# A factorization-machine tower on one core: the last K-tile of field pairs goes into spare rows and one fp32r product

## The reference, cut to what matters

```python
x0 = xk = e                      # (1024, 39, 16)
for W in (f0, f1, f2):           # (39*39, 128), (128*39, 128), (128*39, 128)
    z = einsum('bfd,bgd->bfgd', x0, xk).reshape(b, f*g, d)
    cur = einsum('bpd,pm->bmd', z, W)
    outs.append(cur); xk = cur
z = sum(concatenate(outs, 1), -1)            # (1024, 384)
h = relu(concatenate([z, dense_ctx], 1) @ W_top1 + b_top1)
h = relu(h @ W_top2 + b_top2)
y = h @ W_top3
```

## Time and profile before

| | |
|---|---|
| three runs | 1340.83, 1345.21, 1346.58 us (median 1345.21) |
| the profiled execution, its own time | 1342.32 us |
| its span in the trace | 1340.6 us |
| TensorE busy | 1273.5 us, 95% |
| VectorE, ScalarE, GpSimd busy | 1080.1, 1050.1 and 662.9 us |
| granted TensorE clock, mean over the span | 0.985 |

### The profile page before, as it was taken

How to read it: one execution, slowest core, us unless ns; L and a number is a source line. 1 busy time by engine, 2 the same in 40 slices (tenths; PEclk the granted TensorE clock), 3 DMA queues, 4 the chain that set the end, 5 groups by cost and what they waited for, 6 DMA issues and landing times. The chain is left out here.

```text
span 1340.6 us, 21409 instructions
## 1 busy us (share of the span) xinstructions
PE 1273.5 (95%) x6680; PEld 978.8 (73%) x6680; DVE 1080.1 (81%) x2285; ACT 1050.1 (78%) x3363; POOL 662.9 (49%) x634
## 2 busy tenths in 40 slices
PE   1389999999999999999999999999999999999998
PEld 0347777777777777777777777877777777777787
DVE  2059989988889888788878888798887888788884
ACT  2048888888888888788878888888887888788884
POOL 7777556654545547454566545455474532333100
PEclk9679999999999999999999999999999999999999
DMA  6082012100311003110211103111031102110000
GB/s 142 11 235 54 26 52 73 52 28 3 99 32 44 28 22 91 47 32 14 73 51 51 29 4 94 36 44 29 17 92 51 31 13 70 49 49 27 1 1 1
DMA packets 51178, 63.60 MB, mean 47 GB/s; under 512 B 13068, under 2 KB 24345, under 8 KB 51020
## 3 DMA queue, kind: packets, MB, share of 16 engines
q1 hardware_dynamic: 34544, 56.08, 13.7%
q0 software_dynamic: 10128, 2.98, 2.1%
q10 hardware_dynamic: 6392, 3.18, 1.0%
HBM read 11.08 MB, written 1.02 MB: 9 GB/s over the span
## 5 line engine op out<-in xcount | busy, mean ns | idle before, releaser
L538 ACT ACTIVATE scaled_x<-Y,x_col 128x128 f32<-128x128 f32 x3072 | 929.7, 506 | 190.6 <-PE Y L844 178.7
L842 PE MATMUL Y<-f_high,cur_high 128*128 128x512 f32 (+1 forms) x1280 | 603.7, 472 | 3.7 <-DVE sum_b L688 2.0
L843 PE MATMUL Y<-f_low,cur_high 128*128 128x512 f32 (+1 forms) x1280 | 499.0, 390 | 0.0
L844 PE MATMUL Y<-f_high,cur_low 128*128 128x512 f32 (+1 forms) x1280 | 499.0, 390 | 0.0
L427 POOL TENSOR_TENSOR pairs<-shifted,base 117x512 f32<-117x512 f32 x186 | 241.7, 1301 | 436.6 <-PE C L770 434.7
L688 DVE SCALAR_TENSOR_TENSOR sum_a<-Y,x_col,sum_a 128x128 f32<-128x128 f32 x768 | 264.9, 345 | 155.4 <-PE Y L844 153.3
L391 POOL DMA_INDIRECT rows<-in_tbl_dram,ids_sb x312 | 306.9, 984 | 77.5 <-issue 66.2
L842 PEld LDWEIGHTS Y<-f_high,cur_high 128*128 128x128 f32 x1280 | 241.3, 189 | 95.9 <-issue 37.5
L843 PEld LDWEIGHTS Y<-f_low,cur_high 128*128 128x128 f32 x1280 | 242.1, 189 | 86.3 <-issue 52.1
L707 DVE TENSOR_REDUCE cur<-scaled_x 128x128 f32<-128x1920 f32 x128 | 275.6, 2153 | 15.0 <-ACT scaled_x L538 1.6
L844 PEld LDWEIGHTS Y<-f_high,cur_low 128*128 128x128 f32 x1280 | 240.7, 188 | 51.0
(11 more groups left out here) (90 smaller groups left out, 728.7 us busy)
## 6 DMA issues: line engine op xcount, KB each, us to landing
shifted<-x_seq SPq DMA_DIRECT2D x157, 234.0 KB
base<-x_seq SPq DMA_DIRECT2D x95, 78.0 KB
rows<-in_tbl_dram,ids_sb POOLq DMA_INDIRECT x312
shifted<-x_seq SPq DMA_DIRECT2D x31, 156.0 KB
G<-in_L_rec_f_dram ACTq DMA_DIRECT2D x3, 832.0 KB, 11.8
w_sb<-in_W_top_dram SPq DMA_DIRECT2D x1, 768.0 KB
f_ext<-in_L_rec_f_dram SPq DMA_DIRECT2D x1, 760.5 KB
w_sb<-in_W_top_dram SPq DMA_DIRECT2D x1, 512.0 KB
```

The source lines that it names most:

```text
L538: ins = act.activation(scaled_x[:, :, PLACE[c] + i], where[:, i * M:(i + 1) * M], ACT.Copy, scale=x_col[:, t // JT % QG, t % JT, f:f + 1])
L842: pe.matmul(where, ch, wh, start=True, stop=False)
L843: pe.matmul(where, ch, wl, start=False, stop=False)
L844: pe.matmul(where, cl, wh, start=False, stop=True).then_inc(y_filled, 1)
```

## The change

The pairs of distances 6 and 13, the seventh K-tile, are dealt out anew for groups 1 to 31 (group 0 stays as it was). A K-tile has 117 rows where 128 fit. So 11 spare rows (EXTRA) in K-tiles 1 to 4 take 11 + 6 + 11 + 11 = 39 of the 78 pairs (the second of the four has zero weights in five rows). The other 39 pairs become one fp32r product of 3 * 39 = 117 rows (`left_x` against `f0_left`): high times high, low times high and high times low of the same pairs stand in three bands of rows of one product.

- SP issues per group 3 base copies and one of 11 rows, 5 shift copies and four of 11 rows, 6 copies of 22, 15 and 2 rows for the left pairs (behind k = 2) and, behind everything and a wait for these six (`left_copied`), 4 copies of 39 rows that repeat them in the other two bands. That is 23 in place of 9.
- GpSimd makes `left_products` ahead of pair 3 in tile 1, and `left_low` behind it; pairs 4 and 5 follow in tile 2. ScalarE makes `left_high` behind slot 16 (chunk 6 of tile 1), waiting for `left_made`. The left product is the fourth of the seven sums, at slot 22, and TensorE waits there for `left_low_ready`.
- Group 1's copies now wait until all seven first pairs are made.
- The start loads 26 more small pieces of f0 and prepares `f0_left` on VectorE. `cur1`'s ring has 6 tiles in place of 8, and `z2` and `y` lie inside `h2` and `h1`.

```diff
@@ -38,6 +38,32 @@
+EXTRA = P - SEL
+EXTRA_AT = {1: K0 - 1, 2: NF - K0 + 1, 3: 2 * K0 - 1, 4: NF - 2 * K0 + 1}
+EXTRA_NEW = {1: EXTRA, 2: K0 - 1, 3: EXTRA, 4: EXTRA}
+LEFT_RUNS = [(0, EXTRA, NF - EXTRA - K0 + 1, K0 - 1),
+             (NF - EXTRA - K0 + 1, EXTRA, NF - 2 * EXTRA - 2, 2 * K0 - 1),
+             (NF - 2, NF - 2, 2, 2 * K0 - 1 - NF)]
+LEFT = 3 * NF
+LEFT_COPIES = 2 * len(LEFT_RUNS) + 4
+KT = K0 - 1
+ROWS = [P if k in EXTRA_AT else SEL for k in range(KT)]
+LEFT_AT = 3
...
@@ -59,12 +85,13 @@
 AT_SUM = [13 + 3 * k for k in range(K0)]
 AT_X = 5
+AT_LEFT_HIGH = 6
...
-CUR1_RING = 2 * JT
+CUR1_RING = JT + 2
...
@@ -281,6 +316,17 @@
+            for k, d in EXTRA_AT.items():
+                n = EXTRA_NEW[k]
+                eng.dma_start(f0_sum[SEL:SEL + n, k, :],
+                              bass.AP(f0_ext.tensor, d * M, [[(EXT + 1) * M, n], [1, M]])).then_inc(f0_in, 16)
...
+            for row, f, n, d in LEFT_RUNS:
+                for i, first in enumerate((EXT * f + f + d, EXT * (f + d) + f)):
+                    for j in range(3):
+                        eng.dma_start(left_f0[j * NF + row:j * NF + row + n, i, :],
...
@@ -342,18 +389,32 @@
-                elif g == 2:
+                else:
                     sp.wait_ge(first_pairs, K0)
                 for j in range(BLK):
                     base_copy(sp, g, j)
-                for k in range(1, K0):
+                sp.dma_start(base[SEL:P, g % 2, :], cols[0:EXTRA, :]).then_inc(based[g % 2], 16)
+                for k in range(1, KT):
                     if g >= 2:
-                        sp.wait_ge(pairs_ready, K0 * (g - 2) + k + 1)
-                    else:
-                        sp.wait_ge(first_pairs, k + 1)
+                        sp.wait_ge(pairs_ready, KT * (g - 2) + k + 1)
                     shift_copy(sp, g, k)
+                    if k in EXTRA_AT:
+                        at = EXTRA_AT[k]
+                        sp.dma_start(shifted[SEL:P, k - 1, :], cols[at:at + EXTRA, :]).then_inc(copied[k - 1], 16)
+                    if k == 2:
+                        if g >= 2:
+                            sp.wait_ge(left_low_ready, g - 1)
+                        for row, f, n, d in LEFT_RUNS:
+                            sp.dma_start(base_left[row:row + n, :], cols[f:f + n, :]).then_inc(left_copied, 16)
+                            sp.dma_start(left_pairs[row:row + n, :], cols[f + d:f + d + n, :]).then_inc(left_copied, 16)
+                sp.wait_ge(left_copied, 16 * LEFT_COPIES * (g - 1) + 32 * len(LEFT_RUNS))
+                for j in (1, 2):
+                    rows_j = slice(j * NF, (j + 1) * NF)
+                    sp.dma_start(base_left[rows_j, :], base_left[0:NF, :]).then_inc(left_copied, 16)
+                    sp.dma_start(left_pairs[rows_j, :], left_pairs[0:NF, :]).then_inc(left_copied, 16)
...
@@ -415,17 +476,27 @@
+            def left_products(g):
+                pool.wait_ge(left_copied, 16 * LEFT_COPIES * g)
+                pool.tensor_tensor(left_pairs, left_pairs, base_left[:], ALU.mult).then_inc(left_made, 1)
+
+            def left_low(g):
+                pool.wait_ge(left_high_ready, g)
+                pool.tensor_tensor(left_x[0:NF, :], left_pairs[0:NF, :], left_x[0:NF, :].bitcast(F32), ALU.subtract)\
+                    .then_inc(left_low_ready, 1)
...
@@ -453,10 +524,15 @@
-                    ks = ((0, 1, 2), (3, 4), (5, 6), ())[j] if g + 1 < NG else ()
+                    ks = ((0, 1, 2), ("left", 3, "low"), (4, 5), ())[j] if g + 1 < NG else ()
...
@@ -513,6 +589,12 @@
+            def left_high(g):
+                act.wait_ge(left_made, g)
+                if g >= 2:
+                    act.wait_ge(cur0_summed, K0 * (g - 1) + LEFT_AT + 1)
+                act.activation(left_x[:], left_pairs, ACT.Copy).then_inc(left_high_ready, 1)
...
@@ -576,6 +658,8 @@
+                        if j == 1 and c == AT_LEFT_HIGH and g + 1 < NG:
+                            left_high(g + 1)
...
@@ -702,8 +796,8 @@
-                if j == 0 and g >= 2:
-                    dve.wait_ge(s_filled, S_USE["G", g - 2] + 1)
+                if t >= CUR1_RING:
+                    dve.wait_ge(s_filled, S_USE["G", (t - CUR1_RING) // JT] + 1)
...
@@ -758,17 +852,24 @@
+                if g and i == LEFT_AT:
+                    pe.wait_ge(left_low_ready, g)
+                    if g == 1:
+                        pe.wait_ge(left_f0_ready, 4)
+                    w, x = f0_left[:], left_x[:]
                 else:
...
+                    r = ROWS[k] if g else K0_ROWS[k]
+                    w, x = f0_sum[0:r, k, :], pairs[0:r, RING_USE[g, k] % RING, :]
+                pe.matmul(C[:], w, x, start=i == 0, stop=i == K0 - 1).then_inc(cur0_summed, 1)
```

More of the change, by code:

```diff
@@ L35, with ring_uses @@
 RING = 3
+EXTRA = P - SEL
[9 more added lines that the diff above has]
+LEFT_AT = 3
+STEP = {k: k if k < LEFT_AT else k + 1 for k in range(KT)}
+def ring_uses():
+    uses = [(0, k) for k in range(K0)] + [(g, k) for g in range(1, NG) for k in range(KT)]
+    return {u: n for n, u in enumerate(uses)}, [K0 * g + (STEP[k] if g else k) for g, k in uses]
+RING_USE, READ_BY = ring_uses()
 CH = 10
@@ L200, in build @@
         x_seq = sb("x_seq", [SEQ, 2, P, D])
-        base = sb("base", [SEL, 2, GN])
-        shifted = sb("shifted", [SEL, K0 - 1, GN])
-        pairs = sb("pairs", [SEL, RING, GN])
+        base = sb("base", [P, 2, GN])
+        base_left, left_x = sb("base_left", [LEFT, GN]), sb("left_x", [LEFT, GN], F32R)
+        shifted = sb("shifted", [P, K0 - 1, GN])
+        left_pairs = shifted[0:LEFT, K0 - 2, :]
+        pairs = sb("pairs", [P, RING, GN])
         cur0_high = sb("cur0_high", [P, 2, GN], F32R)
@@ L372, in _ @@
             sp.wait_ge(y_ready, 1)
-            sp.dma_start(out[B - P:B, :].rearrange("b o -> o b"), y[:]).then_inc(y_out, 16)
+            sp.dma_start(out[B - P:B, :].rearrange("b o -> o b"), y).then_inc(y_out, 16)
             sp.wait_ge(y_out, 32)
@@ L455, in _ @@
                             take_rows(bt + 1, part)
-                    ks = ((0, 1, 2), (3, 4), (5, 6), ())[j] if g + 1 < NG else ()
+                    ks = ((0, 1, 2), ("left", 3, "low"), (4, 5), ())[j] if g + 1 < NG else ()
                     for i in range(max(len(ks), len(fs))):
                         if i < len(ks):
-                            pair(g + 1, ks[i])
+                            if ks[i] == "left":
+                                left_products(g + 1)
+                            elif ks[i] == "low":
+                                left_low(g + 1)
+                            else:
+                                pair(g + 1, ks[i])
                         if i < len(fs):
@@ L610, in _ @@
             dve.memset(f0_mirror[0:NF, 0, :], 0.0).then_inc(mirror_zero, 1)
+            for zero in (f0_sum, f0_mirror):
+                dve.memset(zero[96:P, 2, :], 0.0).then_inc(mirror_zero, 1)
             dve.memset(z_dense[:], 0.0).then_inc(dense_zero, 1)
@@ L759, in scalars, with cur0_sum @@
                 ins.then_inc(s_filled, 1)
-            def cur0_sum(g, k):
-                z = K0 * g + k
-                if k == 0 and g:
+            def cur0_sum(g, i):
+                if i == 0 and g:
                     pe.wait_ge(c_read, C_USE["sum", g])
-                if g:
-                    pe.wait_ge(pairs_ready, z - K0 + 1)
-                else:
[L768 to L771, removed]
+                if g and i == LEFT_AT:
[3 more added lines that the diff above has]
+                    w, x = f0_left[:], left_x[:]
+                else:
+                    k = i if not g or i < LEFT_AT else i - 1
+                    if g:
+                        pe.wait_ge(pairs_ready, KT * (g - 1) + k + 1)
+                    else:
+                        pe.wait_ge(first_pairs, k + 1)
+                    r = ROWS[k] if g else K0_ROWS[k]
+                    w, x = f0_sum[0:r, k, :], pairs[0:r, RING_USE[g, k] % RING, :]
+                pe.matmul(C[:], w, x, start=i == 0, stop=i == K0 - 1).then_inc(cur0_summed, 1)
             def bank_free(use):
@@ L816, in mlp1 @@
                     pe.matmul(C[:, w], w1_sb[:, 1, w], g_half(bt)[:, NF, :], start=False, stop=False)
[L817 removed]
+                    ins = pe.matmul(C[:, w], w1_sb[:, 2, w], z2, start=False, stop=True)
                 if ms[-1] == 3:
```

62 lines of the change are left out of this document (41 added, 21 removed).

## The result

| | before | after |
|---|---|---|
| median | 1343.68 us (4 runs, 1340.83 to 1346.58) | 1365.08 us (4 runs, 1359.17 to 1370.42) |
| ratio of the times, 95% interval | | 1.0157 (1.0128 to 1.0186) |
| the profiled execution | 1342.32 us | 1359.17 us |
| granted TensorE clock, mean | 0.985 | 0.975 |

The change makes the kernel 1.6% slower. The runs of after are spread over 11 us, those of before over 6.

What follows compares the result with a forecast made beforehand. TensorE was taken as the bound from the first chunk to the tail. The terms gave 1342.3 - 19 - 1.5 + 24 + 4 = 1349.8, named as 1351 us, with a whole range of 1321 to 1362.

Steps and rivals of the forecast that it cites:

- The product: TensorE's left product in fp32r costs 0.24 us in place of 0.85, saving 19 us over 31 groups.
- The small copies: SP's copies of 11 rows or fewer take 0.80 us each to issue, like the larger ones.
- The rival that they are cheap: SP's small copies at 0.40 us leave the chain nearly in time, giving 1323 us; chance 0.30.
- part-way case: SP's small copies take 0.5 to 0.7 us, part of the way to cheap; chance 0.10.
- The late chain: At hand-overs between batch tiles, late second-stage copies make TensorE wait for GpSimd's low half; 24 us lost at groups 4 to 28.
- Group 1 and the start: Group 1's copies behind all first pairs: its late chain loses 4 us, the earlier fourth-pair copy gains 1.5.
- the term for the clock: TensorE's granted clock after stalls: the sum adds no us for a fall.
- late chains *with the clock held: The forecast's own case: TensorE stands at the hand-overs without a clock fall, 1344 to 1357 us; chance 0.38.
- the rival that takes it down: Each of eight late sums halves TensorE's clock for a while, 1.75 us each, 14 in all: 1365 us; chance 0.20.

Runs made afterwards that it cites:

- both edits: Changed kernel with GpSimd's pair 3 ahead of the left products and SP's second-stage copies right behind k = 3; 1322.94 us, ratio 0.9849.
- the fp32 one: Changed kernel with zeros for the left pairs (their copies, products and halves removed) and the left product in fp32, not fp32r; 1341.54 us, ratio 0.9988.
- the first kernel with delays: both edits plus 7, 9, 10, 12, 13, 15, 18 needless GpSimd instructions ahead of the low half at groups 4, 8, ... 28; 1366.50 us.
- the third with delays: both edits plus needless GpSimd instructions ahead of the low half, 5 in group 4 and 8 in each of groups 8 to 28; 1346.18 us.

## Why the prediction was wrong

- **The product.** Right: 19 us forecast, 19.9 measured by the change of type alone, 0.24 for a product.
- **The small copies.** Right: 0.80 each, measured 0.73 to 0.87 for 11 to 22 rows, 0.59 to 0.64 for 2. The rival that they are cheap had 0.40 with its part-way case; it is refuted, by SP's rows.
- **The late chain.** Right in its steps. It had T + 20.1 for the landing (measured start of the left products T + 20.4) and T + 26.3 for the low half (T + 26.6). Stalls: 3.3 forecast at groups 8 to 24, 3.05 to 3.90 measured; 6 and 5.69 at group 4; 1.5 and 0.68 at group 28. Sum of the seven: 24 forecast, 24.1 measured. GpSimd's wait ended with the second-stage copies, TensorE's with GpSimd, in eight places and no other. The Trainium skill (DMA: Bandwidth & Descriptors, Anatomy of one DMA) gives a fit for the GpSimd path, by which such a copy was estimated at 2.2 us. The copies, issued by SP, needed 2.5 (group 24) to 3.0 (group 16), so the row was the better guide.
- **Group 1 and the start.** Both terms are off, by 3.5 us together, and mostly not for the reason given. The first chunk came 3.0 earlier, where 1.5 was forecast, but the fields were there 3.0 earlier, ahead of anything that the move of group 1's copies can do. The move itself brought the fourth pair 0.8 closer to the fields (15.5 us behind them, before 16.3), and the clock's fall at 81.1, when the first chunks ran, took that back. So that 1.5 was forecast and 3.0 measured is no support for the term. Group 1 lost 1.98, where 4 was forecast: its chain took 26.1, as forecast, but it began at 76.20 and not at the 80.0 that I had taken from the kernel before, 3.0 of that by the fields again.
- **The step that failed** is the term for the clock, which the sum holds at nothing. In "How the numbers follow" late chains *with the clock held* are the likeliest case, at 0.38, against 0.20 for the rival that takes it down. By my own rows the chain gave 3.3 us, and the start's stall of 3.85 had the clock at 0.50 beside it, so "near that one" argued for the rival. Measured: a stall of 3.05 to 3.90 took the clock down at four of five groups, and group 4's of 5.69 did too. These five falls cost 10.4 us and the one at the start 1.15. The rival had 14, for a fall behind each of eight late sums; three of the eight had none, so that its 1365 agrees with the median is in part luck. The sum with the 11.7 is 1349.8 + 11.7 = 1361.5; the start and group 1 take 3.5 off, the tail adds 1.6, which makes 1359.6, and the profiled execution had 1359.17. The Trainium skill says that an idle array falls back to 1.2 GHz (TensorE: Matmul & The Clock Gate, Part 1). This trace agrees at five of its six stalls of 3.05 us and more.
- **The range** ended at 1362 because I closed it at "near the clock's case", though that case, with half the forecast's chance, stood at 1365. The profiled execution lies inside it and the median 5.9 higher. The profiles show only one execution each, so where these 5.9 come from stays open. Other falls behind the stalls would do it, but kernels without any of these stalls spread too: both edits over 1.2 us, the one without the left chain over 3.1, the fp32 one over 7.8 (10 runs), and the kernel before over 7.5 (the 26 runs made with the experiments). The time of the kernel before goes with its mean clock: three runs with 0.997 took 1339.93 to 1340.49, four with 0.992 took 1346.19 to 1347.42. Its seven other runs below 0.99 took 1341.52 to 1347.05; a stretch of 0.50 from about 29 to 57 us, in which TensorE mostly waits for the gathers (busy 4.0 of 27.2 us in before's trace), lowers the mean, and some traces have it and some not. After's runs of 1359.17, 1363.09, 1370.42 and 1367.07 have 0.975, 0.975, 0.976 and 0.979, so the means do not settle it.

## What to carry to other kernels

Where TensorE is the bound, a step taken off it is worth its full time only if the chain that feeds the step ends before its slot at the tightest hand-over: write that chain out from the moment its source is ready, since three copies on SP (2.4 us) and one product with its gather on GpSimd (2.4 us) decided here between 1.6% slower and 1.5% faster. Price a stall of 3 us on a busy TensorE at 4.5 to 6 and not at 3 (an estimate from the 1.5 to 3.0 that a fall cost here), because the products behind it may run at half clock. When a good change measures slower, look at which wait is new and move the work before dropping the change.

## What the runs showed of the hardware

**The length of a stall does not settle its price.** A fall of the granted clock behind a stall lasts 3.4 or 6.8 us in these traces, and costs 1.5 to 1.7 us or 2.6 to 3.0. One of 6.8 us cost only 1.7: at group 24 of the first kernel with delays it began 3.3 us ahead of the left sum, and so lay half in the stall itself. Stalls of 2.19 us at the same place gave one fall in three; 3.63 (after, group 16) and 3.46 gave none, 3.05 gave one of 6.8 us. What besides the length decides I leave open.

**The tail has such falls too**, which the prediction did not price. When the last chunks are done TensorE stands for VectorE's last sum, and then runs 78 products of the third round. Before, and then after:

```profile
1324.03 0.30 PE L799 MATMUL C<-x_block,cur 32*128 32x80 f32 x1 [2.20 <-DVE cur L707]
...
1325.22 8.95 PE L806 MATMUL C<-G,f_sb 128*128 128x128 f32 x78 [0.73 <-ACT G L521]
```

```profile
1339.26 0.30 PE L900 MATMUL C<-x_block,cur 32*128 32x80 f32 x1 [2.21 <-DVE cur L801]
...
1340.45 10.57 PE L907 MATMUL C<-G,f_sb 128*128 128x128 f32 x78 [0.73 <-ACT G L603]
```

The same wait (2.20 and 2.21), the same products, 1.62 us longer. From the last chunk to the end of the span it is 21.9 us in two of the eleven profiles (before and the third with delays), where the clock stayed at 1.00; 23.6 in six with a fall of 3.4 us; 24.6 to 24.9 in three with one of 6.8 us. So up to 3 us between two executions can be the tail's clock and nothing of an edit.

**SP's time for a copy from SBUF to SBUF goes by the copy and not by its rows**: 0.73 to 0.87 us for 11 to 117 rows in the rows above, apart from the one of 1.23. Splitting 39 rows into 22, 15 and 2 costs nearly three copies (0.73 + 0.78 + 0.64). So spare rows are cheap to compute (22 of the 23 groups without a stall are 0.61 to 0.69 shorter, with 11 rows more in four K-tiles) and not cheap to fill.
